# Attention on one core: one score pair, all maximum products, the other score pair, then whole output products of the step before

## The reference, cut to what matters

```python
q = q * cos + _rotate_half(q) * sin          # 8 heads of 8 features
k = k * cos + _rotate_half(k) * sin          # 4 heads, each used by 2 query heads
scores = einsum('bhqd,bhkd->bhqk', q, k) / sqrt(HD)
scores = scores + causal                     # -inf above the diagonal
attn = softmax(scores, axis=-1)
out = einsum('bhqk,bhkd->bhqd', attn, v)
```

## Time and profile before

| | |
|---|---|
| median of three runs | 5339.56 us |
| profiled execution, its own time | 5347.1 us |
| its span | 5345.5 us |
| TensorE (PE) busy | 4621.0 us, 86% |
| TensorE weight loads (PEld) busy | 1664.4 us, 31% |
| VectorE (DVE) busy | 4160.2 us, 78% |
| ScalarE (ACT) busy | 3543.1 us, 66% |
| GpSimd (POOL) busy | 629.7 us, 12% |

### The profile page before, as it was taken

One profiled execution on the slowest core, in us unless ns is written; L12 is line 12 of the kernel. 1 busy time (PEld: TensorE's weight loads), 2 busy tenths in 40 slices (PEclk: granted clock), 3 DMA queues, 4 the chain that ended last, 5 costly groups with the idle time before them and its releaser, 6 DMA issues. The chain is left out here.

```text
span 5345.5 us, 109237 instructions
## 1 busy us (share of the span) xinstructions
PE 4621.0 (86%) x42956; PEld 1664.4 (31%) x42956; DVE 4160.2 (78%) x4691; ACT 3543.1 (66%) x7169; POOL 629.7 (12%) x1092
## 2 busy tenths in 40 slices
PE   8898986599999989999998999999899999965466
PEld 3443433133333233333332333333233333321122
DVE  5555555799989979998997999899799989964511
ACT  3344332188788878888887887887788788742133
POOL 2222222010010010001001000100110010012100
PEclk9999998599999989999998999999899999987688
DMA  3222122200010010001001000100100010024233
GB/s 108 67 67 71 57 66 73 62 12 8 6 36 10 6 32 12 8 6 37 8 6 34 10 8 6 38 8 6 34 10 8 6 38 8 6 66 140 67 104 100
DMA packets 168439, 194.27 MB, mean 36 GB/s; under 512 B 53452, under 2 KB 128380, under 8 KB 167036
## 3 DMA queue, kind: packets, MB, share of 16 engines
q1 hardware_dynamic: 167940, 187.49, 12.6%
HBM read 105.18 MB, written 81.36 MB: 35 GB/s over the span
## 5 line engine op out<-in xcount | busy, mean ns | idle before, releaser
L776 DVE TENSOR_REDUCE part_max<-max_scores 128x2 f32<-128x1024 f32 (+5 forms) x3208 | 3340.8, 1103 | 326.7 <-PE max_scores L740 229.5
L892 ACT ACTIVATE probs<-scores 128x512 f32<-128x512 f32 (+4 forms) x6272 | 3000.7, 538 | 610.6 <-PE scores L922 509.7
L946 PE MATMUL out_acc<-probs,v_keys 128*32 128x256 f32 (+2 forms) x23424 | 1788.0, 377 | 0.0
L740 PE MATMUL max_scores<-k_rows,q_rows 48*128 48x512 bf16 (+5 forms) x6416 | 1188.0, 370 | 216.5 <-DVE part_max L776 144.2
L922 PE MATMUL scores<-q_rows,k_rows 50*128 50x512 bf16 (+4 forms) x6272 | 1211.2, 354 | 88.2 <-ACT probs L892 44.0
L872 POOL TENSOR_SCALAR_AFFINE_SELECT probs<-probs 128x256 f32<-128x256 f32 (+1 forms) x832 | 336.1, 404 | 3485.6 <-ACT probs L892 3483.2
L740 PEld LDWEIGHTS max_scores<-k_rows,q_rows 48*128 48x128 bf16 (+1 forms) x6416 | 314.2, 94 | 1363.5 <-DVE part_max L776 860.5
L946 PEld LDWEIGHTS out_acc<-probs,v_keys 128*32 128x32 f32 x23424 | 462.8, 108 | 741.5 <-issue 621.3
L922 PEld LDWEIGHTS scores<-q_rows,k_rows 50*128 50x128 bf16 x6272 | 459.7, 94 | 424.6 <-ACT probs L892 237.7
L507 DVE SCALAR_TENSOR_TENSOR gated<-gate,x_pad 128x448 f32<-128x448 f32 x252 | 260.9, 1073 | 68.9 <-ACT gate L475 55.9
L446 PE MATMUL token_ps<-gated,w_sb 128*128 128x448 f32 x504 | 234.7, 556 | 33.0 <-DVE gated L507 33.0
(11 more groups left out here) (119 smaller groups left out, 1966.1 us busy)
## 6 DMA issues: line engine op xcount, KB each, us to landing
q_terms_dram<-q_st SPq DMA_DIRECT2D x174, 112.0 KB
q_rows<-q_terms_dram SPq DMA_DIRECT2D x180, 96.0 KB, 2.2
v_keys<-v_blocks_dram SPq DMA_DIRECT2D x18, 832.0 KB, 9.1
v_blocks_dram<-v_st SPq DMA_DIRECT2D x26, 512.0 KB, 3.4
k_rows<-k_terms_dram SPq DMA_DIRECT2D x36, 306.0 KB, 6.6
k_terms_dram<-k_st SPq DMA_DIRECT2D x174, 56.0 KB
x_in<-in_x SPq DMA_DIRECT2D x5, 1568.0 KB, 6.2
h_dram<-h SPq DMA_DIRECT2D x28, 224.0 KB, 2.0
```

The lines of the kernel that those rows point to most:

```text
L740: last = nc.tensor.matmul(max_scores[0:m, n % M_RING, v, 0:keys], q_rows[rows, g, op[3], q0:q0 + m], k_rows[rows, (u // BU) % STEP_B, g, k ...
L776: nc.vector.tensor_reduce(part_max[0:m, u % 2, i, :, p, c], max_scores[0:m, n % M_RING, :, 0:keys], AX_X, ALU.max).then_inc(max_used, 1)
L892: nc.scalar.activation(probs[0:keys, k % P_RING, s, o:width[t]], scores[0:keys, (GH * k + s) % S_RING, o:width[t]], ACT.Exp, scale=float(H ...
L946: last = nc.tensor.matmul(out_acc[VW * s:VW * s + VW, lo:hi], v_keys[0:keys, u // BU, g, j, v * VW:(v + 1) * VW], probs[0:keys, k % P_RING ...
```

## The change

TensorE's order within a step is written anew, in the tensor block of the attention loop. `outputs` loses its argument `part` and always multiplies all columns of a step, in four products instead of eight. The loop over steps issues score pair 0, then all slots of the step, then score pair 1, then the output products of step k - 1. The signals are the same; each is given once per step as before. The number of slots, their distribution over steps, all buffers and the work of the other engines do not change.

```diff
                                              q_rows[rows, g, p, begin[t] + o:begin[t] + width[t]],
                                              start=True, stop=True).then_inc(s_ready, 1)
 
-                    def ends(k):
-                        return k + 1 == first_step[STEPS[k][0] + 1]
-
-                    def outputs(k, part):
+                    def outputs(k):
                         u, j = STEPS[k]
                         g, t = UNITS[u]
                         o = max(0, j * P - begin[t])
                         keys = min(P, S - j * P)
-                        if part == 0:
-                            pe.wait_ge(p_ready, GH * (k + 1))
-                            if k in DIAGONAL:
-                                pe.wait_ge(p_masked, 2 * (DIAGONAL.index(k) + 1))
-                            if j == 0 and u >= 1:
-                                pe.wait_ge(o_copied, u)
-                        middle = max(o, width[t] // 2)
-                        lo, hi = ((o, middle), (middle, width[t]))[part]
-                        if lo < hi:
-                            for s in range(GH):
-                                v = s % GKV
-                                last = nc.tensor.matmul(out_acc[VW * s:VW * s + VW, lo:hi],
-                                                        v_keys[0:keys, u // BU, g, j, v * VW:(v + 1) * VW],
-                                                        probs[0:keys, k % P_RING, s, lo:hi],
-                                                        start=(j == 0 and part == 0), stop=ends(k),
-                                                        skip_group_check=True)
-                            if part == 1:
-                                last.then_inc(p_used, 1)
-                        if part == 1 and ends(k):
+                        pe.wait_ge(p_ready, GH * (k + 1))
+                        if k in DIAGONAL:
+                            pe.wait_ge(p_masked, 2 * (DIAGONAL.index(k) + 1))
+                        if j == 0 and u >= 1:
+                            pe.wait_ge(o_copied, u)
+                        end = k + 1 == first_step[u + 1]
+                        for s in range(GH):
+                            v = s % GKV
+                            last = nc.tensor.matmul(out_acc[VW * s:VW * s + VW, o:width[t]],
+                                                    v_keys[0:keys, u // BU, g, j, v * VW:(v + 1) * VW],
+                                                    probs[0:keys, k % P_RING, s, o:width[t]],
+                                                    start=(j == 0), stop=end)
+                        last.then_inc(p_used, 1)
+                        if end:
                             pe.wait_ge(p_used, k + 1)
                             nc.tensor.sem_inc(o_ready, 1)
 
                     for k in range(len(STEPS)):
                         ops = slots_at[k]
-                        cut = len(ops) // 2
                         score_pair(k, 0)
-                        if k >= 2 and not ends(k - 2):
-                            outputs(k - 2, 1)
-                        for op in ops[:cut]:
+                        for op in ops:
                             run_slot(op)
                         score_pair(k, 1)
                         if k >= 1:
-                            outputs(k - 1, 0)
-                            if ends(k - 1):
-                                outputs(k - 1, 1)
-                        for op in ops[cut:]:
-                            run_slot(op)
-                    if not ends(len(STEPS) - 2):
-                        outputs(len(STEPS) - 2, 1)
-                    outputs(len(STEPS) - 1, 0)
-                    outputs(len(STEPS) - 1, 1)
+                            outputs(k - 1)
+                    outputs(len(STEPS) - 1)
             clear_step()
```

## The result

The changed kernel takes 5631.76 us (median of 4 runs, 5627.48 to 5637.22) against 5342.29 for the kernel before in the same comparison: ratio 1.0544, 95% interval 1.0525 to 1.0562. That is 289 us slower; 328 was forecast.

A forecast was written before the change was run, and what follows sets the result against it. The order of waits was taken as the bound, TensorE standing between VectorE's reductions and ScalarE's exponentials, no engine having much room. Terms summed to 91 us per pass, less 9, times four passes: +328, giving 5668 us; range 5530 to 5815.

The forecast's parts named there:

- why 2.24 is also a latency: Two-slot step before: second pair waits for the first exponential, 1.13 us, exactly filled by TensorE's 1.11; step 2.24.
- (2): Two-slot steps: no output work between the pairs, TensorE stands 0.44 us, whole output follows; step 2.44 against 2.24.
- VectorE's debt: Two-slot steps behind a long one already wait for VectorE before the change; 9 us per pass taken off the sum.
- (3): Slots in a row with two buffers: three-slot step's third product waits for the first reduction; 3.48 us against 2.93.
- (1): Output products of 512 columns take 1.00 us instead of 1.14, since a fixed 0.15 per group is saved.
- (7): First steps of a unit: ScalarE's copy of the finished sums bounds them and stays in place; change 0.
- (4): Wide steps with a transposition of a unit's maxima: eight cost 0.1 us more, six 1.0; 6.8 per pass.
- (6): Narrower steps on the diagonal: longer chain with a whole output, +0.17 us each, 80 steps, 13.6 per pass.
- Rival B: TensorE's pauses lower its clock; a tenth of the loop so would cost 190 us more, 5860; chance 0.11.
- A: Slower by the chain alone: the three-slot wait is absorbed as VectorE catches up in the next step; 5543 us, chance 0.17.
- C: Faster: the wait at the second pair does not bind and TensorE's 0.22 less work shows; 5240 us, chance 0.04.
- D: No change: one wait is exchanged for another of the same length; chance 0.03.

The follow-up runs named there:

- short exponentials: Changed kernel with each exponential over only the first half of its columns (output not the reference's): 5510.34 us, ratio to before 1.0318.
- divided slots: Changed kernel with half the maximum slots ahead of the second pair, the rest behind the whole, late output products: 5871.75 us, ratio 1.0983.
- shorter reductions: Changed kernel with each maximum reduction over only the first half of its keys (output not the reference's): 5424.98 us, ratio to before 1.0158.

## Why the prediction was right

The direction and the two main mechanisms were right. That the total came so near (289 for 328) is in part luck: several terms were off in opposite directions, and one cost was not in the sum at all, as follows.

**The chain of the two-slot step** (its parts "why 2.24 is also a latency" and (2)) held to 0.01 us: 2.45 for 2.44. The short exponentials show that the exponential is in it; the divided slots show that it takes 1.13 even with one slot between the pairs. The difference per step was less than forecast, 0.17 for 0.20 in the mean, because the steps of before took 2.305 in the mean and not the 2.24 of the earlier trace rows. The 9 per pass taken off for VectorE's debt was meant to cover this; the wide two-slot steps show 4.4 of it, and the rest of the 9 happened to stand in for terms that were wrong elsewhere.

**The row of slots with two buffers** (3) held: 3.46 for 3.48, and 2.93 for 2.95 with shorter reductions. It makes 28.5 of the 74.7 us per pass.

**The whole outputs** (1): the value 1.00 was right and its reason wrong. The 0.15 is paid once for outputs in a row, not for each group.

**The first steps** (7) were priced at zero, and that was the term most off: -10.4 per pass. The sum was never worked out for them. By the timelines above four exponentials at about 0.49 and the copy at 0.47 give 2.4, which is what they take now; the 2.71 of before had a gap in ScalarE's work that is gone in the new order. More than that is paid in the second step: +0.50 there against -0.37, 28 times a pass, so first and second steps together grew by 3.7 per pass. **The transposition steps** (4) were over by 6.6 per pass.

**The narrow steps** (6) were under by 3.4: those of 128 columns grew from 1.23 to 1.59, not by 0.17.

**Rival B, the clock**, happened in small. In the loop the granted clock is 0.97 against 0.98. One such place, TensorE in a second step with three slots:

```profile
2361.31 0.39 PE L740 MATMUL max_scores<-k_rows,q_rows 48*128 48x512 bf16 x2 [0.35 <-DVE part_max L776]
...
2362.43 0.46 PE L740 MATMUL max_scores<-k_rows,q_rows 48*128 48x512 bf16 x2 [0.74 <-DVE part_max L776]
...
2362.68 0.64 PE L922 MATMUL scores<-q_rows,k_rows 50*128 50x512 bf16 x2
2363.25 0.20 PEld L940 LDWEIGHTS out_acc<-probs,v_keys 128*32 128x32 f32 x8 [0.70 <-issue]
2363.25 1.94 PE L940 MATMUL out_acc<-probs,v_keys 128*32 128x512 f32 x8
...
2365.12 0.61 PE L922 MATMUL scores<-q_rows,k_rows 50*128 50x512 bf16 x2
```

After two waits for reductions the whole output takes 1.87 to the next pair instead of 1.00, that is 1.2 GHz (1.85 was forecast for it). By the clock records of the two traces TensorE was at this lower level for 244 us of the loop, in 29 stretches, against 114 us in 5 stretches before. Most of the new ones last 3.4 us, and 15 of the 16 steps of 448 columns with four or more slots are touched by one: these are the kind of step that went from 4.00 to 5.28. A step is half as long again at the lower level (3.72 for 2.44 by the forecast's sum, an output 1.87 for 1.00 here), so about a third of the 130 us more, some 43 us, is the clock's. Steps at the upper level throughout grew by 242 us in sum, where all steps grew by 299, which makes it 57. Both are estimates, and no run tested the clock by itself. The forecast's sum had nothing for it, so without the clock the kernel would have lost about 240 us where 328 was forecast.

The Trainium skill (TensorE: Matmul & The Clock Gate, "A second HAM failure mode: psum-queue depth-cycling") says that short idle times between groups of matmuls can make the clock swing between its levels. The trace of the changed kernel agrees, with the 29 stretches above.

**Rivals A, C and D** fell: the third slot's wait was not absorbed (3.46 for 2.93), and the wait at the second pair did bind (the 0.41 of the weight load).

## What to carry to other kernels

When an engine alternates between two partners, the work between two dependent pairs is a cover: count, for each half of the step, the partner's round trip and what stands beside it, before moving anything. Fewer and longer instructions saved at most 27 us here, because what counted was where they stood. And spread a second stream's work by time, not by size: that alone gave 1.1%.

## What the runs showed of the hardware

Two groups of four fp32 products of 256 columns behind one another take as long, 1.00 us, as one group of 512, though a group of 256 followed by a bf16 product takes 0.57: about 0.14 us are paid once for a row of such products, not for each group. TensorE's clock fell to its lower level inside the loop after waits of 0.35 and 0.74 us that stood close together, and stood there for 3.4 us; it was at that level for 244 us of the changed loop and for 114 us of the loop before.
